# One load for the conditioning data and the first batch's x_t, and an earlier first eviction

## The reference, cut to what matters

```python
scale = cond @ norm_w.T + 1.0                       # 32 batches x 256
ms = mean(x * x, -1)
h = x * (scale[:, None, :] * rsqrt(ms + 1e-6))      # x: 32 x 256 x 256
val, gate = split(h @ up_w.T, 2)                    # up_w: 2048 x 256
h = val * gelu(gate)
y = act_quant(h) @ weight_quant(down_w).T + x       # down_w: 256 x 1024
```

## Time and profile before

| | |
|---|---|
| median of 3 runs | 426.77 us (426.59 to 426.85) |
| the profiled execution | 426.46 us, of which the span is 424.7 us |
| TensorE busy | 420.3 us (99% of the span), 2089 products |
| VectorE, ScalarE, GpSimd busy | 279.4, 187.9, 165.2 us |
| chain that ended last | 96% TensorE, 1% each DMA, VectorE and ScalarE |

### The profile page before, as it was taken

The page is one execution under the profiler, slowest core; times in us unless marked ns, Lnnn a source line. Parts: engine busy times, 40 slices in busy tenths (PEclk is TensorE's granted clock), DMA queues, the critical chain, the costliest instruction groups (busy, mean ns, idle before and its releaser), DMA issues.

```text
span 424.7 us, 7679 instructions
## 1 busy us (share of the span) xinstructions
PE 420.3 (99%) x2089; PEld 337.4 (79%) x2089; DVE 279.4 (66%) x538; ACT 187.9 (44%) x335; POOL 165.2 (39%) x323
## 2 busy tenths in 40 slices
PE   8999999999999999999999999999999999999997
PEld 6778888888888788888888887888888888878786
DVE  4986656756657657567566576565675565765676
ACT  6764344444344443444443444434444434444541
POOL 2644443443434434434424344334344243343320
PEclk9999999999999999999999999999999999999999
DMA  8523444333443424443334434244433344342324
GB/s 271 203 54 111 115 99 121 101 79 94 123 99 99 115 71 111 99 121 102 80 93 124 99 100 119 67 109 99 123 99 78 95 124 99 100 120 68 83 51 125
DMA packets 82088, 45.01 MB, mean 106 GB/s; under 512 B 68256, under 2 KB 68768, under 8 KB 81952
## 3 DMA queue, kind: packets, MB, share of 16 engines
q1 hardware_dynamic: 81792, 44.60, 40.3%
q10 hardware_dynamic: 288, 0.33, 0.3%
HBM read 20.00 MB, written 8.39 MB: 67 GB/s over the span
## 4 chain that ended last, share of the span: by engine, by line
PE 96%; DMA 1%; DVE 1%; ACT 1%; SPq 0%; issue 0%; POOL 0%; DVEq 0%; POOLq 0%
PE p_gate L768 41%; PE p_val L768 41%; PE p_y L788 13%; DMA up_raw<-up_w_t 1%; DVE up_lo L487 0%; PE p_val L746 0%; ACT up_hi L376 0%; DVE y_sb L531 0%; PE p_val L752 0%; PE p_val L747 0%; PE p_gate L788 0%; SPq L223 0%; ACT gelu L386 0%; DVE h L496 0%; DVE y_sb L668 0%
## 5 line engine op out<-in xcount | busy, mean ns | idle before, releaser
L625 DVE SCALAR_TENSOR_TENSOR h<-p_val,rstd,gelu 128x512 f32<-128x512 f32 x124 | 92.4, 745 | 128.0 <-PE p_val L768 127.1
L426 ACT ACTIVATE gelu<-p_gate,rstd 128x512 f32<-128x512 f32 x124 | 84.9, 685 | 142.7 <-PE p_gate L768 135.6
L299 POOL TENSOR_TENSOR mean_sq_eps<-mean_sq,rms_eps 128x1 f32<-128x1 f32 x64 | 12.2, 190 | 234.2 <-ACT squares L360 234.2
L372 ACT ACTIVATE q<-q_rounded 128x1024 bf16<-128x1024 f32 x63 | 66.6, 1057 | 77.9 <-DVE q_rounded L592 77.9
L768 PE MATMUL p_gate<-up_hi,a_lo 128*128 128x512 f32 x248 | 80.6, 406 | 0.0
L768 PE MATMUL p_val<-up_hi,a_hi 128*128 128x512 f32 x248 | 78.2, 396 | 0.0
L768 PE MATMUL p_val<-up_hi,a_lo 128*128 128x512 f32 x248 | 78.1, 396 | 0.0
L768 PE MATMUL p_val<-up_lo,a_hi 128*128 128x512 f32 x248 | 78.1, 396 | 0.0
L768 PE MATMUL p_gate<-up_hi,a_hi 128*128 128x512 f32 x248 | 78.1, 396 | 0.0
L768 PE MATMUL p_gate<-up_lo,a_hi 128*128 128x512 f32 x248 | 78.1, 395 | 0.0
L578 DVE TENSOR_REDUCE h_max<-h 128x1 f32<-128x1024 f32 x63 | 76.5, 1215 | 1.2
(11 more groups left out here) (87 smaller groups left out, 250.0 us busy)
## 6 DMA issues: line engine op xcount, KB each, us to landing
xt_in<-x_t SPq DMA_DIRECT2D x32, 256.0 KB, 2.8
x_all<-x SPq DMA_DIRECT2D x32, 256.0 KB, 2.9
out<-y_sb SPq DMA_DIRECT2D x31, 256.0 KB, 2.0
up_raw<-up_w_t SPq DMA_DIRECT2D x7, 256.0 KB, 5.3
down_raw<-down_w_t SPq DMA_DIRECT2D x1, 1024.0 KB, 7.9
q_t<-q SPq DMA_TRANSPOSE x63, 3.1
up_raw<-up_w_t ACTq DMA_DIRECT2D x1, 256.0 KB, 2.9
out<-y_sb SPq DMA_DIRECT2D x1, 128.0 KB, 2.0
```

Of the source, the lines that this page charges most:

```text
L299: pool.tensor_tensor(mean_sq_eps[:, j:j + 1], mean_sq[:, j:j + 1], rms_eps[:, :], ALU.add).then_inc(pool_step, 1)
L372: act.activation(q[j % 2][:, :], q_rounded[j % 2][:, :], ACT.Copy, bias=-ROUND).then_inc(q_ready, 1)
L426: act.activation(gelu[c][:, :], p_gate[c][:, :], ACT.Gelu, scale=rstd[:, j:j + 1]).then_inc(gelu_done, 1)
L625: nc.vector.scalar_tensor_tensor(h[s][:, c * W:(c + 1) * W], p_val[c][:, :], rstd[:, j:j + 1], gelu[c][:, :], op0=ALU.mult, op1=ALU.mult). ...
```

## The change

The conditioning data and the first batch's `x_t` stand side by side in one input of 2688 B a partition (640 B and 2048 B), loaded by one transfer into `first_sb`, and everything that used either waits for `first_landed`. `xt_in[0]` is used from batch 2 on, so GpSimd's wait counts one transfer less there and SyncE's wait for `first_a_ready` is gone. Beside that, ScalarE makes high part (2,1) before the first gelu, and VectorE makes the first `h` before low part (3,0).

```diff
-        cond_norm_sb = sb("cond_norm_sb", [KD * C, B + P], fp32)
+        first_sb = sb("first_sb", [P, B + P + KD * 2 * P], fp32)
+        cond_norm_sb = first_sb[:, 0:B + P]
+        first_xt = first_sb[:, B + P:].rearrange("p (k j q) -> p k j q", k=KD, j=2)
...
-            sp.dma_start(cond_norm_sb[:, :], cond_norm).then_inc(cond_norm_in, 16)
-            load_xt(0, 0)
+            sp.dma_start(first_sb[:, :], first_in).then_inc(first_landed, 16)
             load_up(0, 1)
...
-            sp.wait_ge(first_a_ready, KD * TPB)
             load_xt(1, 0)
...
-                    if j % TPB == 0:
+                    if j == 0:
+                        pool.wait_ge(xt_landed[0], 16 * u)
+                    elif j % TPB == 0:
                         pool.wait_ge(xt_landed[j // TPB], 16 * (u + 1))
...
-            act.wait_ge(xt_landed[0], 16)
+            act.wait_ge(first_landed, 16)
...
             high_part(2, 0)
+            high_part(2, 1)
             early_gelu(0, 0)
-            high_part(2, 1)
             high_part(3, 0)
...
-            dve.wait_ge(xt_landed[0], 16)
+            dve.wait_ge(first_landed, 16)
...
             low_part(2, 1)
+            early_h(0, 0)
             low_part(3, 0)
-            early_h(0, 0)
             low_part(3, 1)
...
             keep_busy(13)
-            pe.wait_ge(cond_norm_in, 16)
+            pe.wait_ge(first_landed, 16)
```

More of the change, by code:

```diff
@@ L26, with build @@
 P = 128
-def build(nc, x, x_t, cond_norm, up_w_t, down_w_t, out):
+def build(nc, x, x_t, first_in, up_w_t, down_w_t, out):
     fp32, fp32r, bf16, i16 = mybir.dt.float32, mybir.dt.float32r, mybir.dt.bfloat16, mybir.dt.int16
@@ L35, in build @@
     TPB = x.shape[2]
-    C = cond_norm.shape[0] // 2
+    C = first_in.shape[0] // 2
     KD = D // P
@@ L121, in build @@
         down_in = sem("down_in")
-        cond_norm_in = sem("cond_norm_in")
+        first_landed = sem("first_landed")
         xt_landed = [sem(f"xt_landed{i}") for i in range(2)]
@@ L392, in _ @@
             high_part(0, 0)
-            act.wait_ge(xt_landed[0], 16)
+            act.wait_ge(first_landed, 16)
             for k in range(KD):
                 act.wait_ge(scale_ready, k + 1)
-                act.activation(a_hi[1][:, k, :], xt_in[0][:, k, 1, :], ACT.Copy,
+                act.activation(a_hi[1][:, k, :], first_xt[:, k, 1, :], ACT.Copy,
                                scale=scale_t[:, k, 0:1]).then_inc(second_a_hi_ready, 1)
@@ L467, in _ @@
                                         ALU.add).then_inc(scale_ready, 1)
-            dve.wait_ge(xt_landed[0], 16)
+            dve.wait_ge(first_landed, 16)
             for k in range(KD):
                 dve.wait_ge(scale_ready, k + 1)
-                nc.vector.tensor_scalar(a_hi[0][:, k, :], xt_in[0][:, k, 0, :], scale_t[:, k, 0:1], None,
+                nc.vector.tensor_scalar(a_hi[0][:, k, :], first_xt[:, k, 0, :], scale_t[:, k, 0:1], None,
                                         ALU.mult).then_inc(a_hi_ready, 1)
@@ L479, in x_low_part @@
                     dve.wait_ge(second_a_hi_ready if t else a_hi_ready, k + 1)
-                    nc.vector.scalar_tensor_tensor(a_lo[t][:, k, :], xt_in[0][:, k, t, :], scale_t[:, k, 0:1],
+                    nc.vector.scalar_tensor_tensor(a_lo[t][:, k, :], first_xt[:, k, t, :], scale_t[:, k, 0:1],
                                                    a_hi[t][:, k, :].bitcast(fp32),
@@ L855 @@
     tokens = np.ascontiguousarray(x).reshape(B, P, TPB, D)
+    x_t = np.ascontiguousarray(tokens.reshape(B, P, TPB, KD, P).transpose(0, 4, 3, 2, 1))
+    cond_norm = np.concatenate(
+        [np.concatenate([np.asarray(cond_256).T, np.asarray(L0_cond_norm_w).T[:, k * P:(k + 1) * P]], axis=1)
+         for k in range(KD)], axis=0)
     laid = {
         "x": tokens,
-        "x_t": np.ascontiguousarray(tokens.reshape(B, P, TPB, KD, P).transpose(0, 4, 3, 2, 1)),
-        "cond_norm": np.ascontiguousarray(np.concatenate(
-            [np.concatenate([np.asarray(cond_256).T, np.asarray(L0_cond_norm_w).T[:, k * P:(k + 1) * P]], axis=1)
-             for k in range(KD)], axis=0)),
+        "x_t": x_t,
+        "first_in": np.ascontiguousarray(np.concatenate([cond_norm, x_t[0].reshape(P, -1)], axis=1)),
         "up_w_t": np.ascontiguousarray(
```

## The result

The changed kernel takes 428.08 us (median of 8 runs, 427.50 to 428.69), the kernel before beside it 426.64 us (426.57 to 426.85): a ratio of 1.0032, 95% interval 1.0023 to 1.0041. It is slower, where 0.34 us less was forecast, and lies outside the range of 425.9 to 427.0. The profiled execution took 428.23 us with a span of 426.4 us.

What follows compares the result with a forecast made beforehand. TensorE, busy 99% of the span, was taken as the bound: a fixed block of work behind a start. Exchange -0.41 and merged load +0.07 sum to -0.34 us, likeliest 426.43 us, range 425.9 to 427.0.

Steps and rivals of the forecast that it cites:

- The merged load: Kernel start: one load for conditioning data and `x_t` makes the scale product later; cost +0.07 us.
- L: Landing time of the merged load at the kernel start, taken as 4.25 us, between bounds of 3.95 and 4.6.
- Clock: TensorE's first gate products: a standstill before the scale product leaves them at half speed; not in the forecast sum.
- case 5: Standstill before the scale product keeps TensorE slow for another 2.86 us: +1.35 us, 427.8 us; chance 0.04.
- products of `first_gate` 0.43 us apart: Sign at TensorE's first gate products: the prediction is wrong if they stand 0.44 us apart.
- Transfer: Start loads: the gate product after TensorE's standstill (the restart) was forecast at 6.28 us instead of 6.10.
- L + 0.73: Time by which high part (0,0) must be done to cost nothing, since ScalarE waits for the scale until then.
- The rule that the prediction cited against the change: First load and piece (0,0) would land together near 4.6 us: case 3, 426.8 us, chance 0.18.
- The exchange: Two reordered steps at the start: first `h` runs earlier, removing TensorE's wait at the first value part; -0.41 us.
- Case 4: Low part (3,1) or the gelu slips past its cover; a new wait leaves -0.1 us, 426.6 to 426.8; chance 0.06.

Runs made afterwards that it cites:

- merge-only: The changed kernel with the two exchanged steps put back, so the merged load alone, against the kernel before: medians 426.72 and 427.82 us, ratios 1.0011 and 1.0019.

## Why the prediction was wrong

- **The merged load, "+0.07 us", in general L - 4.18.** This is the step that failed. L was right to 0.02 us, the price wasn't. In the profiled execution it is 1.33 + 1.00 = +2.33 us, of two parts: the clock, which the sum put at nothing, and the late piece (0,0).
- **Clock, +1.63 us of it** against merge-only's trace at the high level (restart at 7.43 instead of 6.80, and 1.00 behind it), 1.20 us against the profiled execution with 16 fillers (428.23 and 427.03), and 0.65 us between the medians of one session. The prediction named it as case 5, with its place, 1.35 us for it and 427.8 as the time, and gave it 0.04, because standstills of 0.3 us had left the spacing alone in one execution. Those standstills ended at 5.06 and 6.10, behind the halving at about 3.5 us, so they say nothing on one that comes while the level is still low. And one trace can't give the odds of that, since the moment differs from run to run: about 3.5 us in the trace of before, between 5.3 and 5.8 and at 6.3 in those of the exchange alone, 8.8 to 9.9 in the three of the changed kernel and the second of merge-only. One of the signs that the prediction named for being wrong is there, products of `first_gate` 0.43 us apart. Filling the gap drew the runs together at 427.0, and less filling in the kernel before gave the loss without a change of loads.
- **Transfer, +0.70 us** where 0.18 was worked out for the restart. "High part (0,0) may be late ... it costs nothing as long as it is done by L + 0.73" was the right condition, but (0,0) landed at 5.0 to 5.3, 0.7 to 1.0 us after the merged load and past L + 0.73, so `a_hi[1]` and high part (0,1) queued behind it on ScalarE. The bigger load held the other queue's back by 1.2 us. The rule that the prediction cited against the change, that each engine takes packets in turn from the queues that have work (the Trainium skill's "DMA: Bandwidth & Descriptors", "Queues, rings and completion order"), is not what this case's traces show: the queues were served largely one after the other, and the two loads did not end together at 4.6, but the merged one at 4.25 and the piece at 5.1. The same page's estimate for the size, from "Anatomy of one DMA" in the Trainium skill, L = 3.5, was too early by 0.75.
- **The exchange, -0.41 us**, was right as a mechanism: no wait on `h` in the changed kernel or in either trace of the exchange alone. It was wrong as a term to be added. It pays only while the restart is punctual, and the merged load spends it: in merge-only's profiled execution the restart is 0.70 us late and the loop's first product only 0.30 (17.40 instead of 17.10), since the cushion took 0.41 of it. That execution took 426.60 us, the one before 426.46.
- Case 4, a new wait in the old one's place, did not occur in the changed kernel, where the late start gave low part (3,1) time. It did in the second trace of the exchange alone and in those with 16 and 19 fillers (0.12 to 0.41 us): its cover of 0.17 us was too thin for the 0.06 that it was given. The loop was untouched, six products in 1.40 us.
- **The calibration.** A tenth of the chance was left outside the range, and the only case on the slower side got 0.04. It deserved the weight of a mechanism whose trigger, a TensorE standstill before the first real products, the change was itself forecast to create (3.6 to 4.3 us). That case 5's 427.8 lies near the median of 428.08 is partly luck, for the late piece (0,0) was no part of it.

Still open is what sets the moment. The level rose inside a gap of 1.21 us in one execution and inside one of 0.41 in another, while it had not risen at the end of gaps of 0.44 to 0.60 in four others. The traces don't show why. Nor is the standstill separated from the number of fillers, since both changed together in all runs but one, the scale product that waits for `x_t`; there the trace has no slow stretch, and the three slower runs weren't profiled.

## What to carry to other kernels

Merging two loads takes away the early landing of the smaller one. Ask what fills the engine that used it, and what the larger first load does to the load on the other queue; here both cost more than the issue saved. A standstill of TensorE before its spacing has halved is not priced by its length: it can leave a stretch of products at half speed, and one trace of the kernel before doesn't show the odds. A standstill behind that moment says nothing on it. A wait found on the critical path may be a cushion for lateness ahead of it; before adding its removal to a sum, look at what else lands there, and which step becomes the next wait.

## What the runs showed of the hardware

TensorE's spacing halves at a moment that differs between executions of one kernel. The 14 traces fall into three kinds:

- No gap between the first fillers and the scale product: halved between 3.5 and 6.3 us (five traces).
- A gap, but the high level there when it ended (gaps of 0.41, 0.64 and 1.21 us): the moment fell into the gap twice, and before it once; nothing slow came behind (three traces).
- A gap, and still the low level when it ended (gaps of 0.30 to 1.69 us): halved only between 8.4 and 9.9 us (six traces).

The Trainium skill says that the moment varies, in "TensorE: Matmul & The Clock Gate", the part on the HAM clock gate: the monitor runs on its own and does not restart with the kernel, so the number of slow products varies from run to run. The traces agree that it varies.

The granted clock in the tables reads 1.00 all through the slow stretch, so it is the spacing of equal products that shows the level. The odds differ by session: merge-only had six runs of 11 at 426.72 or under in the first, and three of 11 under 427 in the second.
